# Attention block of a macaron layer: column-tiled q/k/v products, residual side on GpSimd, second PV sums copied by VectorE

## What is computed

```python
x = x + 0.5 * ffn(layernorm(x))
x = x + attn(layernorm(x))
x = x + 0.5 * ffn(layernorm(x))

# attn(y), 4 query heads, 2 key/value heads of 32 values
h = y * rsqrt(mean(y*y) + 1e-6) * norm_w
q, k, v = l2norm(h @ Wq), l2norm(h @ Wk), h @ Wv
a = softmax(causal(q @ k.T * exp(log_temperature)))
attn(y) = y + gate * (a @ v) @ Wo
```

## Time and profile before

| what | value |
|---|---|
| median of 3 runs | 436.24 us (435.81 to 436.36) |
| profiled execution, its own time | 436.85 us |
| its span in the trace | 435.0 us |
| TensorE busy | 397.6 us, 91% of the span |
| VectorE busy | 369.9 us, 85% |
| ScalarE busy | 370.1 us, 85% |
| GpSimd busy | 252.7 us, 58% |
| granted TensorE clock | 0.999 |

### The profile page before, as it was taken

How to read it: one execution, slowest core, us unless ns; L and a number is a source line. 1 busy time by engine, 2 the same in 40 slices (tenths; PEclk the granted TensorE clock), 3 DMA queues, 4 the chain that set the end, 5 groups by cost and what they waited for, 6 DMA issues and landing times.

```text
span 435.0 us, 12717 instructions
## 1 busy us (share of the span) xinstructions
PE 397.6 (91%) x4899; PEld 214.0 (49%) x4899; DVE 369.9 (85%) x943; ACT 370.1 (85%) x497; POOL 252.7 (58%) x325
## 2 busy tenths in 40 slices
PE   0689999899898999999999999999999999999994
PEld 0346666664434445445445445345454345666654
DVE  5889999699799989999989999999769948878554
ACT  4799999776797898898898897998988989999950
POOL 5689999984634526426337247151123558999860
PEclk9999999999999999999999999999999999999999
DMA  6487423606426235037137036046044125654542
GB/s 169 108 189 164 51 51 48 117 7 87 110 55 97 46 70 114 17 69 107 24 74 124 2 74 122 3 96 101 2 79 71 26 49 76 110 131 101 115 103 78
DMA packets 119229, 35.18 MB, mean 81 GB/s; under 512 B 101632, under 2 KB 119168, under 8 KB 119168
## 3 DMA queue, kind: packets, MB, share of 16 engines
q1 hardware_dynamic: 117888, 34.02, 41.3%
q10 hardware_dynamic: 1280, 0.33, 0.3%
HBM read 4.98 MB, written 4.19 MB: 21 GB/s over the span
## 4 chain that ended last, share of the span: by engine, by line
DVE 31%; PE 28%; ACT 16%; issue 12%; POOL 6%; DMA 5%; DVEq 1%; SPq 1%; ACTq 0%
PE ps L507 8%; DVE RD L241 6%; ACT PT L871 5%; DVE X L1080 4%; PE ps L754 4%; ACT XN L459 4%; PE ps L761 4%; PE ps L724 4%; DVE H L328 3%; PE ps L571 3%; PE ps L560 3%; ACT SG L477 2%; DVE AN L1067 2%; POOL HL L434 2%; DVE SS L1086 2%
## 5 line engine op out<-in xcount | busy, mean ns | idle before, releaser
L871 ACT ACTIVATE PT<-ps,k_exp 128x1024 f32<-128x1024 f32 x144 | 153.9, 1122 | 15.0 <-PE ps L724 9.1
L507 PE MATMUL ps<-XT,WT 128*128 128x512 f16 x384 | 93.8, 383 | 6.5 <-DMA XT<-w_int 2.0
L724 PE MATMUL ps<-QKT 128*32 128x512 f16 (+1 forms) x1280 | 86.6, 359 | 4.3 <-DMA QKT<-ST 2.3
L754 PE MATMUL ps<-PT,V 128*32 128x512 f32 (+3 forms) x768 | 76.1, 486 | 2.5 <-ACT PVS L911 2.5
L761 PE MATMUL ps<-PT,ones 128*32 128x512 f32 (+3 forms) x768 | 76.1, 486 | 0.0
L434 POOL TENSOR_TENSOR HL<-H,HH 128x1024 f16<-128x1024 f32 x31 | 66.6, 2149 | 8.5 <-ACT HH L483 5.6
L328 DVE SCALAR_TENSOR_TENSOR H<-SG,k_isilu,ps 128x1536 f32<-128x1536 f32 x32 | 57.9, 1809 | 14.4 <-ACT SG L477 6.3
L507 PEld LDWEIGHTS ps<-XT,WT 128*128 128x128 f16 x384 | 34.4, 98 | 50.8 <-issue 10.4
L1003 POOL TENSOR_TENSOR ST<-QN,ST 128x512 f16<-128x512 f32 x16 | 19.0, 1185 | 64.0 <-ACT ST L903 64.0
L459 ACT ACTIVATE XN<-X,NB,RS 128x128 f32<-128x128 f32 x128 | 52.5, 483 | 2.1 <-POOL NB L406 2.0
L477 ACT ACTIVATE SG<-ps,k_silu 128x1536 f32<-128x1536 f32 x32 | 48.8, 1526 | 4.4 <-DVE H L328 4.3
(11 more groups left out here) (139 smaller groups left out, 646.8 us busy)
## 6 DMA issues: line engine op xcount, KB each, us to landing
result<-X SPq DMA_DIRECT2D x15, 256.0 KB, 2.5
X<-in_L_attn_x SPq DMA_DIRECT2D x7, 512.0 KB, 4.5
X<-in_L_attn_x SPq DMA_DIRECT2D x2, 256.0 KB, 4.4
XT<-w_int SPq DMA_TRANSPOSE x32, 3.1
QKT<-ST SPq DMA_TRANSPOSE x18, 6.1
AXT<-AS SPq DMA_TRANSPOSE x16, 2.8
w_int<-in_L_ffn_w_gate SPq DMA_DIRECT2D x1, 192.0 KB, 4.3
w_int<-in_L_ffn_w_up SPq DMA_DIRECT2D x1, 192.0 KB, 4.4
```

Of the source, the lines that this page charges most:

```text
L507: i = e.matmul(out[:, j, :], WT[:, wp, w * NJ + j, :], XT[k % 2][:, xp, :], start=a == 0, stop=a == len(passes) - 1)
L724: i_ = e.matmul(dst[r, :].rearrange("p (s a n) -> p s a n", a=2, n=P), QKT[k % 2][:, i // TPC, NH + hp, key0 + r.start:key0 + r.stop], q.r ...
L754: e.matmul(sums_of(h, 0, n), V[k % 2][:, i, v0:v0 + HD], weights_of(g, h, o, n), start=i == 0, stop=i >= TPC * qc, skip_group_check=True)
L871: e.activation(dst, SCORES[(SLOT0[g] + i) % 2][:, :, :], ACT.Exp, scale=k_exp[:, 0:1]).then_inc(a_exp, 1)
```

## The change

- TensorE: in the steps, each q/k/v product of 128x128 weights becomes four of 128x32, one on each column tile. The four projections issued before the attention (`k is None`) stay as they are.
- `add_norm` moves from VectorE to GpSimd for chunks 2 to 15 (chunks 0 and 1 stay on VectorE). `wo_out` gets a wait on `a_y`.
- The copy of the second half's PV sums moves from ScalarE at the start of the next step to VectorE at the end of the step (`second_pv_out`).
- ScalarE: the `v_out` of `("qkv", 1, 1)` moves from g 2 to g 3, behind `pv_out` and the exponentials of group 4; in step 0 `stack_hi` of the second half moves from g 8 to g 9, behind the exponentials of the next batch's group 0.
- The run-time loops of VectorE and ScalarE are written out where `shift` is False, GpSimd's always.

```diff
+        def second_pv_out(e, b):
+            e.wait_ge(a_pv, b * NG + NG)
+            e.wait_ge(a_on, 2 * b + 1)
             for i in range(2):
                 e.tensor_copy(PVS[:, i, :], PVD[:, i, :]).then_inc(a_pvc, 1)
...
-                            i_ = e.matmul(dst[:, t * NQKV:(t + 1) * NQKV],
-                                          AXT[half][:, xp, tt * P:(tt + 1) * P],
-                                          QKVO[:, wp, 0:NQKV], start=a == 0, stop=a == 2)
+                            for r in [slice(0, P)] if k is None else COLUMN_TILES:
+                                i_ = e.matmul(dst[r, t * NQKV:(t + 1) * NQKV],
+                                              AXT[half][:, xp, tt * P + r.start:tt * P + r.stop],
+                                              QKVO[:, wp, 0:NQKV], start=a == 0, stop=a == 2)
...
 def att_act
-                    if g == 0 and k >= 1:
-                        pv_out(b * 2 - 1, b * NG)
...
-                        for c, at in enumerate((3, 3) if k == 0 else (1, 2)):
+                        for c, at in enumerate((3, 3) if k == 0 else (1, 3)):
...
-                        if g == 8:
+                        if g == (9 if k == 0 else 8):
                             stack_hi(m0 + 1, 1)
...
 def att_pool
+                if k == 0:
+                    add_norm(e, 2, 2, 2)
+                    add_norm(e, 3, 3, 3)
                 if k >= 1:
                     o_lo(e, b * 2 - 1)
+                if k >= 1 and later:
+                    add_norm(e, m0 + 2, m0 + 2, q)
...
                 if nxt:
                     stack_lo(m0, 0)
+                if k == 0:
+                    add_norm(e, m0 + 2, m0 + 2, q)
+                if later:
+                    add_norm(e, m0 + 3, m0 + 3, q + 1)
                 o_lo(e, b * 2)
...
 def att_dve
             def wo_out(k, b, u, c):
                 src = await_full(e, k, b, u).rearrange("p (t d) -> p t d", t=TPC)
+                e.wait_ge(a_y, c + 1)
...
-            for m in range(2, 4):
-                add_norm(m, m, m)
...
-                if later:
-                    add_norm(m0 + 2, m0 + 2, q)
-                    add_norm(m0 + 3, m0 + 3, q + 1)
...
                 if nxt:
+                    second_pv_out(e, b)
                     wo_out(k, b, ("wo", 0), b * 2)
```

More of the change, by code:

```diff
@@ L183, in macaron_kernel, with drive @@
         block = ctx.enter_context(nc.Block())
-        def drive(eng, step, n, head, tail):
+        def drive(eng, step, n, head, tail, straight=False):
+            if straight:
+                for i in range(n):
+                    step(i, i)
+                return
             for i in range(head):
@@ L243, in o_norm @@
             e.tensor_tensor(ON[:, :], PVS[:, 0, :], RD[:, :], ALU.mult).then_inc(a_on, 1)
-        def last_pv_out(e):
-            e.wait_ge(a_pv, B * NG)
-            e.wait_ge(a_on, 2 * B - 1)
+        def second_pv_out(e, b):
+            e.wait_ge(a_pv, b * NG + NG)
+            e.wait_ge(a_on, 2 * b + 1)
             for i in range(2):
@@ L696, in macaron_kernel, with add_norm @@
         COLUMN_TILES = [slice(c, c + HD) for c in range(0, P, HD)]
+        def add_norm(e, m, c, q):
+            if isinstance(m, int) and m < 2:
+                e.wait_ge(a_fac, 13)
+            else:
+                e.wait_ge(a_coef, 5 * m - 5)
+            e.wait_ge(a_xn, m + 1)
+            for t in range(TPC):
+                i = e.tensor_scalar(tile(c, t), tile(c, t), A1[q][:, t:t + 1], B1[q][:, t:t + 1],
+                                    ALU.mult, ALU.subtract)
+            i.then_inc(a_y, 1)
         def att_pe(e, shift, first=None, head=None):
@@ L848, in step @@
                         use(k, b, u)
[L849 to L853, removed]
+            drive(e, step, B, 1, 3, not shift)
         def projections_read(e, shift):
@@ L961, in step @@
                         x_hi(m0 + 3, 1)
-            drive(e, step, B, 1, 3)
+            drive(e, step, B, 1, 3, not shift)
             e.activation(warm[:, :], lt_t[:, :], ACT.Silu)
@@ L1038, in step @@
                     ffn_pool(e, 1, [("x_hi", 2), ("x_lo", 2), ("rstd", 4)])
-            drive(e, step, B, 1, 3)
+            drive(e, step, B, 1, 3, True)
         def att_dve(e, shift, first=None):
@@ L1070, in normalise @@
                     i.then_inc(a_xn, 1)
[L1072 to L1082, removed]
             def sums(m, half):
@@ L1199, in att_dve @@
                 for m in range(2):
-                    add_norm(m, m, m)
+                    add_norm(e, m, m, m)
                 return
@@ L1257, in step @@
                 if nxt:
+                    second_pv_out(e, b)
                     wo_out(k, b, ("wo", 0), b * 2)
                     rows(m0 + 1, k, b, 1)
-            drive(e, step, B, 1, 3)
-            last_pv_out(e)
+            drive(e, step, B, 1, 3, not shift)
+            second_pv_out(e, B - 1)
             wo_out(B - 1, B - 1, ("wo", 0), 2 * B - 2)
```

## The result

The changed kernel takes **438.42 us** (median of 5 runs, 437.08 to 439.27) beside 435.81 (5 runs, 435.34 to 436.36) of the kernel before on the same chip: ratio 1.0059, 95% interval 1.0036 to 1.0081. It is slower, by about 2.6 us; 430.5 was predicted, with 426.5 to 435 as the range.

The account below looks back on a forecast made before the run. VectorE and ScalarE's order were taken to bound the steady batch, TensorE 4% behind. Gains of 5.0 (four steady windows), 0.6 (next window), 0.1 (last) and 0 (batch 0), 5.7 us in all, turn 436.24 into 430.5; range 426.5 to 435.

Parts of the forecast that it names:

- The place of the second PV copy: End of a batch on VectorE: copies start 3.2 us after `stack_hi`, behind stack_hi2 and two statistics; weigh(0) 0.3 late.
- The waiting falls in part on what stands there instead: VectorE: more than half of the residual side's 5.1 us a batch is waiting for GpSimd, partly passed to its replacements.
- Batch 0: Window 116.26 to 150.14: weigh(0) of batch 1 later by an us or two, saved waits give it back; 0 net.
- GpSimd's tensor_scalar: Residual side on GpSimd: 0.43 us an instruction, from 0.3 to 0.45, eight a batch, 3.4 us, covered by idle stretches.
- Rival D: GpSimd's instructions take about 1 us and block VectorE; PV copies late, TensorE waits at every weigh(0): 445 us; chance 0.11.
- rival A: VectorE stays the bound, as nearly every GpSimd tensor_scalar blocks it: 31.1 us a batch, 434.2 in all; chance 0.16.
- Column tiles: TensorE's q/k/v products: entering and leaving the full-width form, 0.20 us three times a batch, goes; 0.6 us a batch.
- weigh(3): TensorE's wait there for ScalarE's copy falls from 0.72 to about 0.15 us, with `v_out` moved behind `pv_out`.
- Lockstep of ScalarE and TensorE: Groups 4 to 8 of a steady batch, where ScalarE has one more copy: 0.25 us added a batch.
- rival B: TensorE and ScalarE hold each other in groups 4 to 8, 0.5 us a batch over the allowance: 432.5 to 433; chance 0.10.
- Loops written out: The written-out loops, with `wo_out`'s new wait and fewer ScalarE instructions, were to bring 0, hidden.
- The base of 30.1: Length in us, without waits, of the window ending at 306.51, which has no statistics; the steady batch's sum starts there.

Follow-up runs that it names:

- the trial above: The version with early statistics, each GpSimd addition written as two broadcast-operand products of 128x512 instead of four tensor_scalar: 438.74 us.

## Why the prediction was wrong

- **The place of the second PV copy is the step that failed.** "weigh(0) is late by about 0.3" was a wait of 1.0 to 1.35 us in each steady batch, and the copy that was to start 3.2 us after `stack_hi` starts after 4.15. A steady batch is 30.95 us instead of 30.2, 3.0 of the 7.9 us by which the forecast missed. The order was read rightly (stack_hi2, two statistics, copies); what was mis-sized was the 3.1 us from stack_hi2 to the copies, taken from the kernel before, where the residual side standing ahead of it had absorbed the waiting for GpSimd. With it gone, stack_hi2 met `x_lo` and `stack_lo` itself: 1.68 listed instead of 0.49. "The waiting falls in part on what stands there instead" was written down and was not added where it counted. The prediction also took the order for granted instead of seeing that VectorE would idle 1.8 us for `stack_hi` just ahead of the 2.6 us of statistics that then delay the copies. Moving the statistics into that gap gives 430.42 us: the term decided the sign, and most of the 4.3 us of the next point hang on it too.
- **Batch 0 "0, with 1 us either way" was +4.3.** The text names the mechanism (weigh(0) late "by an us or two") and lets the saved waits pay for it. The wait was 3.29 us, and behind it came the half clock, some 1.7 us, of which the prediction had nothing. The "us or two" was counted for the later `stack_hi` alone; GpSimd's additions, which delay the transposes and the low half there (1.06 and 0.80 us), had no term in this batch, though the text says what comes late "if that cover goes". In the version with early statistics the window is 34.76: about 0.9 over that of before, within the bound.
- **GpSimd's tensor_scalar**: 0.43 taken, 0.84 measured, twice the nearest rows. Rival D had the price and the place, TensorE waiting at every weigh(0), but not its mechanism: it made VectorE pay for the length of each. VectorE's timeline beside GpSimd's eight from 117.92 on says otherwise, in two of its two-input instructions of one size:

```profile
118.69 0.18 DVE L1109 TENSOR_TENSOR RT<-RT,R 128x24 f32<-128x24 f32 x1
118.90 0.32 DVE L1111 SCALAR_TENSOR_TENSOR R<-RT,R 128x24 f32<-128x24 f32 x1
```

One in three is lengthened there, by 0.14; the longest such row is 0.40. So the blocking was overestimated as the duration was underestimated, and rival A falls with it. What does hold VectorE is GpSimd's two-input products, those that were there before and the broadcast ones of the trial above. The Trainium skill's sentence (SBUF — State Buffer, Who interferes with whom) that the second to come waits for the whole of the first agrees with 1.19 for 0.21 beside `stack_lo` and with 0.96 for 0.18 beside a broadcast product, and not with the rows beside a tensor_scalar.
- **Column tiles**: the seam went, as predicted; 0.4 us a batch and not 0.6. The Trainium skill's 3.07 (TensorE: Matmul & The Clock Gate, Measured speedup vs the span model), by which the prediction had nothing to gain, is given there for four row tiles. It is not what these column tiles show: 12 groups of four in 1.31 us, 0.11 each, the time of one full-width product.
- **weigh(3)**: the wait was to fall from 0.72 to 0.15 and fell to none; undone, it costs 0.5 a batch. That step held.
- **Lockstep of ScalarE and TensorE, 0.25 a batch (and rival B)**: the 29.66 us batches, with TensorE busy 29.66, leave nothing for it.
- **Loops written out: "0, hidden"** was 1.6 us in the kernel before: 0.45 of the 1.35 us of waiting that the prediction found in a steady batch were the loops'. The sum left it out. What it is worth in the change no run shows.
- The sum itself: 5.0 predicted for the steady batches, 5.4 once the order is changed, and 430.42 beside 430.5. The base of 30.1 held: less 0.4 for the tiles it is 29.7, and the batches without a wait take 29.66. The low end of the range is 426.7 by its own terms (2.8 and one), not 426.5. That the two agree is partly luck, since the loops were left out, the tiles overvalued, and batch 0 still gives back about an us.

That the profiled execution of the change has the span of the one before, 435.0 us, is chance: it was the fastest of its five, and that of before was above its median. So the rows above explain the shape of the change and not all of the 2.6 us. The other four have a mean granted clock of 0.990 to 0.994, the longest of them the lowest; that the two of 0.990 and 0.991 lose more at half clock would fit, but none of the four has rows here.

## What to carry over

When work on a path is handed to another engine, write down the order that the receiving engine will have around it, and ask of each instruction ahead of it who waits for it and when: here 2.6 us of unhurried statistics stood between an idle gap and a copy for which TensorE waited, and the two orders of these lines are 8 us apart. Waiting that a removed instruction absorbed does not vanish; it goes to the next instruction in order, so price that one beside its neighbour and not alone. What helps a unit that is not the bound measures as nothing (the column tiles on the kernel before), and shows its worth when the bound has moved.

## What the runs showed of the hardware

- A GpSimd tensor_scalar of 128x128 f32 with two per-partition operands takes 839 ns (VectorE does eight in 2.13 us) and lengthens VectorE's 128x24 instructions beside it not at all in two cases of three, else by 0.14 to 0.22 us. A product of 128x512 with a broadcast operand takes 1039 to 1084 ns, and holds a two-input instruction of VectorE to its end (0.96 us instead of 0.18). Two of these do the work of four of those in 2.1 us instead of 3.3, and gave the slower kernel by 1.7%.
- Waits of TensorE of 2.5 to 4.1 us at weigh(0) went with 3.4 to 6.8 us at half clock (0.50 granted), which in the two cases of 6.8 us began before the wait ended; those of 1.0 to 1.8 us did not. The length of the wait is not all of it: in the version with batch 0's copies first a wait of 2.54 us has the clock at 1.00 in all windows up to 154 us. Keeping TensorE busy with products that nobody reads held the clock (1.00 instead of 0.50 behind the wait) and gained about 2 us.
- The run-time loops of VectorE, ScalarE and GpSimd cost the kernel before 0.45 us in a steady batch, all of it waits of TensorE for late operands; on VectorE an idle 0.28 us is all that was found.
